# Linear-attention scan: two steps per instruction, projecting products spread behind the sums

## The reference, cut to what matters

```python
# x: tokens after the mixture; per batch b:
q, k, v, g = h @ Wq, h @ Wk, h @ Wv, h @ Wg          # h: layer-normed, modulated x
decay = exp(log_sigmoid(h @ Wgk1 @ Wgk2 + b) / 16)   # per key feature and token
# for each head, key feature d and value column j, over time t:
S[t] = decay[t] * S[t-1] + k[t] * v[t]               # the scan
o[t] = sum over d of q[t] * S[t]
out = rmsnorm(o) * norm_w * silu(g)  ->  @ Wo
```

## Time and profile before

| what | us |
|---|---|
| median of three runs | 2703.91 |
| the profiled execution's own time | 2707.64 |
| its span | 2705.9 |
| PE busy | 2429.1 (90%) |
| DVE busy | 1765.7 (65%) |
| POOL busy | 1101.5 (41%) |
| end of mixture and first projection, from | 1669 |
| first scan / last scan starts | 1790.6 / 2239.0 |
| the 256 scans, each 1.213 | 306.6 busy |

### The profile page before, as it was taken

The page is one execution under the profiler, slowest core; times in us unless marked ns, Lnnn a source line. Parts: engine busy times, 40 slices in busy tenths (PEclk is TensorE's granted clock), DMA queues, the critical chain, the costliest instruction groups (busy, mean ns, idle before and its releaser), DMA issues. The chain is left out here.

```text
span 2705.9 us, 34532 instructions
## 1 busy us (share of the span) xinstructions
PE 2429.1 (90%) x10120; PEld 1644.8 (61%) x10120; DVE 1765.7 (65%) x2613; ACT 1280.7 (47%) x2550; POOL 1101.5 (41%) x1112
## 2 busy tenths in 40 slices
PE   6999979999999996989999995668898876999999
PEld 5778845555555553866888884434444424788877
DVE  4230239999999995776555553679999997511253
ACT  3223039999999994235555552642223213411121
POOL 0112035666666563663000002258998995111110
PEclk9999989999999997989999998789999998999999
DMA  5254435555555544658667763634544455201021
GB/s 181 80 135 171 119 103 171 160 169 178 157 171 178 158 155 139 230 196 282 224 230 228 226 232 114 231 132 155 170 160 164 167 180 171 79 24 47 12 87 65
DMA packets 287526, 421.45 MB, mean 156 GB/s; under 512 B 37816, under 2 KB 120776, under 8 KB 287408
## 3 DMA queue, kind: packets, MB, share of 16 engines
q1 hardware_dynamic: 252656, 369.16, 42.8%
q10 hardware_dynamic: 28704, 33.08, 3.6%
q0 software_dynamic: 6048, 17.75, 2.0%
HBM read 304.11 MB, written 115.82 MB: 155 GB/s over the span
## 5 line engine op out<-in xcount | busy, mean ns | idle before, releaser
L1068 ACT ACTIVATE attn_probs<-attn_ps_score,attn_nmax 128x512 f32<-128x512 f32 x512 | 343.2, 675 | 2.2 <-DVE attn_nmax L1142 2.2
L2662 PE MATMUL scan_ps_o<-scan_qs,scan_sel 128*128 128x512 f32 x512 | 269.2, 646 | 74.2 <-DVE scan_qs L2607 72.0
L2624 DVE TENSOR_TENSOR_SCAN scan_st<-scan_ps_dec,scan_kv 128x512 f32<-128x512 f32 x256 | 306.6, 1213 | 5.7 <-POOL scan_kv L2573 5.6
L975 PE MATMUL attn_ps_score<-attn_KK,attn_X 64*128 64x512 f32 x512 | 213.9, 465 | 21.0 <-ACT attn_probs L1068 20.4
L2662 PEld LDWEIGHTS scan_ps_o<-scan_qs,scan_sel 128*128 128x128 f32 x512 | 90.4, 196 | 225.0 <-DVE scan_qs L2607 150.6
L2205 POOL DMA_INDIRECT gla_vb<-rows_y,row_i x32 | 33.5, 1047 | 464.5 <-POOLq L3313 412.5
L1156 DVE SCALAR_TENSOR_TENSOR attn_mixed<-attn_probs,attn_cf,attn_mixed 128x512 f32<-128x512 f32 x256 | 193.4, 755 | 9.1
L2573 POOL TENSOR_TENSOR scan_kv<-gla_vb,gla_gk 128x512 f32<-128x512 f32 x128 | 160.9, 1283 | 39.6 <-POOLq L2097 33.0
L1131 DVE TENSOR_REDUCE attn_raw<-attn_ps_score 128x2 f32<-128x1024 f32 x128 | 156.5, 1223 | 28.4 <-PE attn_ps_score L975 27.3
L975 PE MATMUL attn_ps_score<-attn_KL,attn_X 64*128 64x512 f32 x512 | 173.0, 423 | 0.0
L975 PE MATMUL attn_ps_score<-attn_KK,attn_Y 64*128 64x512 f32 x512 | 160.3, 398 | 0.8 <-POOL attn_Y L865 0.8
(11 more groups left out here) (559 smaller groups left out, 6859.1 us busy)
## 6 DMA issues: line engine op xcount, KB each, us to landing
gla_vb<-gv SPq DMA_DIRECT2D x256, 256.0 KB
moe_raw<-in_L_ffn_gating SPq DMA_DIRECT2D x92, 512.0 KB
rows_x<-attn_zeros SPq DMA_DIRECT2D x32, 1024.0 KB, 13.4
moe_raw<-in_L_ffn_linear SPq DMA_DIRECT2D x46, 512.0 KB, 4.6
late<-rows SPq DMA_DIRECT2D x32, 384.0 KB, 9.1
attn_spread<-rows SPq DMA_DIRECT2D x32, 384.0 KB, 9.0
moe_xb<-rows_x SPq DMA_DIRECT2D x23, 512.0 KB, 4.8
rows_y<-moe_y ACTq DMA_DIRECT2D x23, 512.0 KB, 6.4
```

The source lines that it names most:

```text
L975: last = nc.tensor.matmul(ps_score[n][:, j, :], weights, y[p][half, :], start=(r == 0), stop=(r == len(terms) - 1))
L1068: nc.scalar.activation(probs[b][:, at_j, :], ps_score[n][:, j, :], ACT.Exp, bias=nmax[b][:, at_j:at_j + 1], accum_out=Z[b][:, at_j:at_j + ...
L2624: V.tensor_tensor_scan(st[r][:, :], ps_dec[n % 2][:, :], kv[r][:, :], 0.0, ALU.mult, ALU.add).then_inc(st_ready, 1)
L2662: nc.tensor.matmul(ps_o[w][:, :], sel[:, P - GPH - GPH * d:2 * P - GPH - GPH * d], qs[i % RING][:, :], start=(d == 0), stop=(d == HALF - 1 ...
```

## The change

In the scan, two steps (a pair) go into one instruction:

- `kv` and `st` are rings of 3 pairs [128, 1024], `qs` of 2 pairs (still 4 slots). POOL makes a pair's kv in one instruction; DVE scans both in one, with the decay twice in PSUM and a 0 at the second half's first column, so that the state starts anew.
- DVE weighs a whole pair in one instruction, or only its first step where POOL weighs the second.
- `ps_dec` takes 4 PSUM banks; `ps_o` becomes one tile, so the first sum of each half group waits until ACT has copied the last one. `rstd` moves from PSUM to SBUF (`osq[:, 1, :]`).
- The 12 matmuls of a projected tile are issued three at a time behind four sums, its evacuation three steps later.
- `finish` goes behind the pair scan of steps 10 and 11, `gate` behind the kv pair of steps 12 and 13, ms behind sum 4, `decay` from e = 30 to 34 (now behind `copy_q`), `log_sigmoid` from 24 to 28.

In the mixture, the first sequence's features: `shifted(0)` comes ahead of two weighings on ACT, `low(0)` ahead of the mixing of tokens 4 and 5 on DVE, the first three evacuations a step earlier, and the first `log_sigmoid` moves from ahead of the second sequence's deviation to behind its features.

```diff
-def gla_product(nc, out, what, j, W, hT, s):
+def gla_product(nc, out, what, j, W, hT, s, part=None):
...
+        if part in (None, k):
+            last = nc.tensor.matmul(out[0:w, :], W[x][:, k, 0:w], hT[y][:, k, :], start=(n == 0), stop=(n == len(passes) - 1))
# mixture, ACT
+                    if b == 1 and t < TT - 1:
+                        evacuate(t)
...
-                    if t:
-                        i = GROUP * (b - 1) + t - 1
-                        evacuate(i)
-                        if GLA_TILES[i] == ("z", 1):
-                            log_sigmoid()
+                    if b > 1 and t:
+                        evacuate(GROUP * (b - 1) + t - 1)
...
-                if b == 0:
-                    for n in range(TT, TT + PER):
-                        weigh(n)
...
                 shifted(b)
+                if b == 0:
+                    for n in range(TT, TT + PER):
+                        weigh(n)
+                if b == 1:
+                    log_sigmoid()
# mixture, DVE
+                    if b == 1 and t == 0:
+                        low(0)
                     mix(b * TT + t)
-                    if b and t == 1:
+                    if b > 1 and t == 1:
                         low(b - 1)
+                        if b == 2:
+                            log_sigmoid()
# scan
+        PAIRS, WEIGHED_PAIRS = 3, RING // 2
-        FINISH_AT = 8
+        FINISH_AT, TILE_LATE, SQUARES_LATE = 10, DC - 1, 1
-        LOG_AT, LESS_AT, DECAY_AT, SQUARES_AT = 14, 24, 30, 3
+        LOG_AT, LESS_AT, DECAY_AT, SQUARES_AT = 18, 28, 34, 4
# POOL
+            def weigh_second(m_):
+                i = 2 * m_ + 1
+                pool.wait_ge(st_ready, m_ + 1)
+                pool.wait_ge(summed, i - RING + 1)
+                G.tensor_tensor(qs[m_ % WEIGHED_PAIRS][:, 1, :], st[m_ % PAIRS][:, T:], gq[b % 2][:, h, :], ALU.mult
+                                ).then_inc(pool_qs_ready, 1)
+            for m_ in range(NB * NV // 2):
+                i = 2 * m_
+                if m_ >= PAIRS:
+                    pool.wait_ge(st_ready, m_ - PAIRS + 1)
+                G.tensor_tensor(kv[m_ % PAIRS].rearrange("p (y t) -> p y t", t=T), vb[:, y:y + 2, :], gk[b % 2][:, h, :].unsqueeze(1).to_broadcast([P, 2, T]),
+                                ALU.mult).then_inc(kv_ready, 1)
+                if m_ and by_pool(i - 1):
+                    weigh_second(m_ - 1)
                 if n and j == FINISH_AT + 2:
                     gate(n - 1)
# DVE
-                    V.scalar_tensor_tensor(out=norm[:, w, :], in0=osb[:, w, :], scalar=nw[:, w:w + 1], in1=ps_rstd[:, :],
+                    V.scalar_tensor_tensor(out=norm[:, w, :], in0=osb[:, w, :], scalar=nw[:, w:w + 1], in1=rstd,
+            def weigh(m_):
+                i = 2 * m_
+                k = 1 if by_pool(i + 1) else 2
+                if i >= RING:
+                    dve.wait_ge(summed, i - RING + k)
+                V.tensor_tensor(qs[m_ % WEIGHED_PAIRS][:, :k, :], st[m_ % PAIRS][:, :k * T].rearrange("p (y t) -> p y t", t=T),
+                                ps_q[:, :].unsqueeze(1).to_broadcast([P, k, T]), ALU.mult).then_inc(qs_ready, 1)
+                V.tensor_tensor_scan(st[m_ % PAIRS][:, :], ps_dec[n % 2][:, :], kv[m_ % PAIRS][:, :], 0.0, ALU.mult, ALU.add).then_inc(st_ready, 1)
+                if m_:
+                    weigh(m_ - 1)
# PE
+                for part in range(DC):
+                    for r in at_step.get(i - part, ()):
+                        if items[r][0] != "ms":
+                            fill(r, part)
# ACT
-                nc.scalar.copy(ps_dec[n % 2][:, :], gdec[b % 2][:, h, :]).then_inc(dec_copied, 1)
+                nc.scalar.copy(ps_dec[n % 2][:, :T], gdec[b % 2][:, h, :]).then_inc(dec_copied, 1)
+                nc.scalar.copy(ps_dec[n % 2][:, T + 1:], gdec[b % 2][:, h, 1:]).then_inc(dec_copied, 1)
```

More of the change, by code:

```diff
@@ L2070, in gla_product @@
     for n, (k, x, y) in enumerate(passes):
-        last = nc.tensor.matmul(out[0:w, :], W[x][:, k, 0:w], hT[y][:, k, :], start=(n == 0), stop=(n == len(passes) - 1))
+        if part in (None, k):
+            last = nc.tensor.matmul(out[0:w, :], W[x][:, k, 0:w], hT[y][:, k, :], start=(n == 0), stop=(n == len(passes) - 1))
     return last
@@ L2448, in linear_attention @@
         lnms = osq[:, 0, :]
-        ps_dec, ps_o, bank = ([m.ps(f"ps_{n}{i}") for i in two] for n in ("dec", "o", "bank"))
-        ps_q, ps_rstd = m.ps("ps_q"), m.ps("ps_rstd")
+        ps_dec, bank = [m.ps(f"ps_dec{i}", (P, 2 * T)) for i in two], [m.ps(f"ps_bank{i}") for i in two]
+        ps_q, ps_o, rstd = m.ps("ps_q"), m.ps("ps_o"), osq[:, 1, :]
         const_ready, nw_in, dec_copied, q_copied, kv_ready, st_ready, qs_ready, summed, o_ready, sq_ready, ln_ready = (
@@ L2635, in _, with fill @@
             pe.wait_ge(const_ready, 6)
-            def fill(r):
+            def fill(r, part):
                 what, j, b = items[r]
-                if r >= 2:
+                if r >= 2 and part == 0:
                     pe.wait_ge(bank_taken, r - 1)
@@ L2650, in fill @@
                     return
+                if what == "z" and part < DC - 1:
+                    return
                 if (what, j) == ("z", 0):
@@ L2653, in fill @@
                 w = None if what == "z" else W[GLA_CHUNKS.index((what, j))]
-                gla_product(nc, bank[r % 2], what, j, w, [s["ghT"][y][:, b - 1, :, :] for y in two], s).then_inc(bank_done, 1)
+                last = gla_product(nc, bank[r % 2], what, j, w, [s["ghT"][y][:, b - 1, :, :] for y in two], s, part)
+                if part == DC - 1:
+                    last.then_inc(bank_done, 1)
             for i in range(NB * NV):
@@ L2691, in take @@
                     act.wait_ge(norm_ready, n * 2)
-                nc.scalar.copy(osb[:, w, :], ps_o[w][:, :]).then_inc(o_ready, 1)
+                nc.scalar.copy(osb[:, w, :], ps_o[:, :]).then_inc(o_ready, 1)
                 act.wait_ge(o_ready, n * 2 + w + 1)
```

100 lines of the change are left out of this document (45 added, 55 removed).

## The result

The changed kernel takes 2712.99 us, the median of ten runs (2709.98 to 2720.8); the kernel before, run beside it, 2706.56 (2698.98 to 2709.26). The ratio is 1.0036, with a 95% interval of 1.0022 to 1.0051: by the ratio 9.7 us slower, between 6 and 14 (the two medians differ by 6.4). The forecast was 2712.1, 8.2 slower. The experiments led to a version at 2675.6, 1.2% faster than the kernel before.

A forecast was written before the change was run, and what follows sets the result against it. PE, DVE and POOL were taken as within 1% of each other, so waits between them count. Scan terms went from 391.5 to 398.7 (+7.2), first group +1.0, mixture 0: +8.2 on 2703.9 gives 2712.1 us, range 2688 to 2720.

The forecast's parts named there:

- Merged passes: DVE and POOL in the scan: pair scan 2.21 us, merged weighing 1.12, DVE's quad 6.12 instead of 6.26.
- light quads: Scan quads (four steps) where nothing but DVE's work binds: 21 of them at 6.12 us.
- first group: The scan's first 16 pairs: -1.5 us from merging, +0.7 for the log, +1.8 for a later kv start; +1.0 in all.
- The ring in time: Scan quads with products: POOL waits for PE's later sum, starting at s + 2.8; 19 quads at 6.48 us.
- Gates: Scan groups' ends: kv pair 7 waits behind finish and gate; seven gates 75.2 us, bounds 66.5 to 84.
- Slow PE: Quads behind gates: PE's lower clock after idling over 2 us costs 1.0; seven at 7.5 us, two at 6.3.
- rival 4: Quads behind gates: PE's slow stretches are paid in full, +6.3 us, 2718.4; chance 0.12.
- Logs: log_sigmoid in the scan waits for a gap in POOL's queue: 3.4 us for 4.95, twice; first group 2.4 for 1.7.
- q and ACT: Scan: copy_q no longer stands behind decay; DVE's 11.4 us of waiting go and nothing takes their place.
- v loads: Scan: a v load comes at least three kv pairs, 7 us, ahead of use; bound 0 to 2 us in all.
- The end: End of the scan: the two last sums stand where one stood behind a POOL weighing; 0 us.
- The mixture: Stage before the scan: ACT and DVE set the pace with the same passes; 0 us, bounds -4.5 and +1.5.

The follow-up runs named there:

- e1: The kernel before with only the changed mixture functions, its scan left as before; 2708.3 us, ratio 1.0016 to the kernel before.
- e3: The changed kernel, but of an odd pair POOL weighs the first step and DVE the second; 2696.5 us, ratio 0.9976 to the kernel before.
- e6: The changed kernel with a tile's twelve products spread otherwise, none between the odd pair's two sums; 2708.3 us, ratio 1.0008 to the kernel before.
- e11: The changed kernel with a tile's twelve products in one block behind its sum, evacuated one step later; 2731.2 us, ratio 1.0087 to the kernel before.
- e7: The changed kernel with finish multiplying by a tile in PSUM in place of rstd in SBUF; 2708.3 us, ratio 1.0013 to the kernel before.
- e4: The changed kernel with kv made one pair further ahead and the gate one pair later; 2689.6 us, ratio 0.9936 to the kernel before.
- e5: The changed kernel with only the gate and the store behind it one pair later; 2713.2 us, ratio 1.0027 to the kernel before.
- e2: The changed kernel with the mixture of the kernel before, so only the scan's change; 2707.5 us, ratio 1.0012 to the kernel before.
- e8: The changed kernel with e3's and e4's edits together and the mixture of the kernel before; 2678.6 us, ratio 0.9897 to the kernel before.
- e10: e8 with finish one pair later and the last pair scanned in two halves behind the preceding pair's weighing; 2691.4 us, ratio 0.9939.
- e9: e8's scan with the changed mixture, ACT's logs moved ahead of the waiting weight split; 2675.6 us, ratio 0.9883 to the kernel before.

## Why the prediction was right, and where it was not

The time and the sign were right, and so was what costs most, the late kv behind PE's sums and behind the gates. That the sum agrees to 1 us is partly luck: the mixture and the end, both put at 0, cost 4.3 us (by e1's ratio) and 3.7, while the scan part came out 3 us shorter than forecast; and the three stretches of the one profile add up to 14.9, not 9.7.

*Merged passes* (right): the pair scan takes 2.28 and 2.20 from start to start (taken: 2.21), the merged weighing 1.11 (1.12), light quads 6.09 (6.12), in 20 places (21). A small slip: 32 x 1.72 is 55.0, not 54.8, so the first group was to win 1.7, not 1.5.

*The ring in time* (right, the best step): 6.52 a quad in 17 places, for 6.48 in 19; POOL's weighing 2.88 behind the scan's start for 2.8. e3, e6 and e11, which move the sum that POOL needs or the products around it, show that this is the cause.

*Gates* (right): 11.67, 10.28, 10.77, 10.28, 10.78, 10.07 and 10.41 make 74.3, against 75.2. e7 shows the port's part: without it the gate of group 2 takes 9.17, but that of group 3, where the finish did not meet POOL, is still 10.7. That the lack of lead is the cause was shown by e4 (with e5 for the other half of its edit); the prediction had that too, but not how cheap the remedy is.

*Slow PE* (place right, spread wrong): five quads behind gates took 8.59, 7.12, 6.96, 8.78 and 8.49, 39.9 against 37.5; in e2, with the same scan, 43.2, paid in full as in rival 4. The granted clock from 1870 to 1880 and from 2040 to 2050 us is 0.83. An idle of over 2 us did not always bring the lower level: behind the gate of group 3 PE idled 2.88 us (to 1988.54), the granted clock stayed at 1.00, and that is the quad of 6.96. In the last sequence there was nothing to pay (6.09, taken 6.3), nor behind the logs beyond the logs themselves.

*Logs* (mis-sized): 1.45, 1.45 and 1.67 in place of 3.4, 3.4 and 2.4, which is 4.6 us. The prediction took it that the log waits until POOL's queue has a gap. It did not:

```profile
1953.40 1.45 DVE L2624 SCALAR_TENSOR_TENSOR gla_gdec<-gla_gdec,gla_gsg 128x1024 f32<-128x1024 f32 x1
```

```profile
1951.40 5.70 POOL L2582 TENSOR_TENSOR scan_kv<-gla_vb,scan_gk 128x1024 f32<-128x1024 f32 x2
```

The first kv pair took 2.38 us, and the second, started behind the log, 3.36 for the usual 2.35: the log got in between two instructions of POOL that stood without a gap. In e8 it did too (2.35, with 5.71 for the two pairs). In the kernel before (5.03, three kv) and in e10 (5.95, two pairs) it had to let all of them pass, though it started first; so "first come first served", as the prediction has it, does not describe these rows. What decides it no run shows.

*q and ACT* (right): the 11.4 went and nothing came in its place. *v loads* (0, bound 2; too low for this profile): 3.8 and 2.9 us of POOL's waits in the last group, and DVE lost 0.66, 1.83 and 1.62 by them, 4.1 in all, which about cancels the logs' 4.6. They come with the slow loads of Wo told above, and e2 and e7, with the same order of loads, have next to none of them.

*The end* (wrong: 0): from the last scan's start to the finish it is 13.2 us, for 9.9 before. The pair scan is 1.1 longer, and four sums stand behind it, 3.70 us, where two stood, 1.98. The prediction counted two, and forgot that the merged weighing of the pair before waits behind the last scan as well. With 0.4 for the longer gate that is +3.7. The part behind the last scan grew by 5.0; the other 1.3 arise between 2258 and 2600 us and stay open (e1, whose scan is the old one, shows 2.0 more there).

*The mixture* (wrong: 0, bounds -4.5 and +1.5): +2.5 to +7.3. I had seen that the weight loads would be issued 1.4 later, and that the logs leave one stretch and come back in another. I had not asked what the logs hid: a wait for weights. Taken out of it they gave little back (the second deviation comes 1.0 and 3.1 us sooner behind the first gather, for 5.9 us of logs), and put elsewhere they cost their 5.8 (28.3 to 28.6 us from the second deviation to the third, 22.5 before).

The test "the first scan more than 3 us away from 1791.7" was hit (1787.29), and rightly says that the mixture was not understood, though it points the wrong way: the start of the stage had moved by 10.6.

## What to carry to other kernels

When instructions are merged, the rings hold the same bytes but fewer hand-overs: draw the loop of who waits for whom with its times, over one round, before counting the saved overhead; here DVE's work fell by 11 us of 1766, and its waits for kv came to 40.5. Give the engine that feeds the others a lead longer than the longest thing that is ever put into its queue; a lead of one pair more, with the gate a pair later (e4), took 27 us off the changed kernel. How much of e9's gain needs the merging was not tested: by the rows the shorter passes give 0.17 a quad, 9.5 us in 56, while the 11.4 of q come from an order that the unmerged kernel could have too, and it was not run with it. Before an instruction is moved away from a wait, ask what the wait is for: work in the shadow of a load is free, and stops being so elsewhere.

## What the runs showed of the hardware

- A DVE instruction with two inputs in SBUF beside POOL's work took up to 4.37 us for two passes of 0.7 (e5's finish at 1921.74, beside a weighing and a kv pair of POOL without a gap between them), and 1.40 to 1.42 with one input in PSUM (e7). A pass over 1024 columns, 1.13 by itself, took 1.45 when it got in between two instructions of POOL and 5.95 when two pairs of kv went ahead of it (e10).
- A scan over a tile that crosses from one PSUM bank into the next, and starts anew by a zero decay, runs no slower than the single ones: 2.20 us from start to start for 1024 columns, 1.14 for 512.
- The same program reaches the mixture at times 13.4 us apart (1656.9 to 1670.4) in fourteen executions of its unchanged part, while the stretches behind it repeat to some 3 us. Comparisons of one profile with another are to be made from a mark inside the stage.
- Loads that are issued alike can take three times as long in another execution: the four loads of Wo landed after 5.0 us in e2 and after 14.2 in the changed kernel, whose scans are the same.
